# An mLSTM and expert-FFN kernel: a wait of its own for each row scatter, and a new order of the last silus and token rows

## The reference, cut to what matters

```python
xn = layernorm(x)
# attention, per sequence and head
q, k, v = headwise(xn, wq), headwise(xn, wk), headwise(xn, wv)
D_mat = exp(log_D - max_log_D)               # from the forget and input gates, causal
C = (q @ k.T / sqrt(dh)) * D_mat
h = (C / (maximum(abs(C.sum(-1)), exp(-max_log_D)) + eps)) @ v
s = multihead_layernorm(h) * (1 + ln_w)
# experts
top1 = argmax(softmax(xn @ router_w + router_b))
for i in range(8):                            # each token keeps its expert's result
    a, g = split(xn @ w1[i] + b1[i])
    y_i = (a * sigmoid(g)) @ w2[i] + b2[i]
out = x + s * silu(y)
```

## Time and profile before

| | us |
|---|---|
| median of 3 runs | 234.85 (234.79 to 235.79) |
| the profiled execution's own time | 235.47 |
| its span, first to last instruction | 233.7 |
| TensorE busy | 217.2 (93% of the span) |
| VectorE busy | 162.4 (69%) |
| ScalarE busy | 140.3 (60%) |
| POOL busy | 92.6 (40%) |

### The profile page before, as it was taken

How to read it: one execution, slowest core, us unless ns; L and a number is a source line. 1 busy time by engine, 2 the same in 40 slices (tenths; PEclk the granted TensorE clock), 3 DMA queues, 4 the chain that set the end, 5 groups by cost and what they waited for, 6 DMA issues and landing times.

```text
span 233.7 us, 6082 instructions
## 1 busy us (share of the span) xinstructions
PE 217.2 (93%) x1824; PEld 173.1 (74%) x1834; DVE 162.4 (69%) x491; ACT 140.3 (60%) x326; POOL 92.6 (40%) x130
## 2 busy tenths in 40 slices
PE   8998989678899889999999999999999999998994
PEld 6787654234545454569999999999999999996541
DVE  5998699507467658755877987798779967963170
ACT  2398758456767676877556655665566555552044
POOL 5667930756566563000333333333433333335100
PEclk9999999976999999999999999999999999999999
DMA  6999999930179111400077021011101001000498
GB/s 180 328 363 418 337 205 210 209 111 34 49 202 327 35 48 44 129 3 28 18 223 255 14 67 57 23 57 56 47 28 52 22 26 35 17 22 13 110 341 267
DMA packets 23617, 29.26 MB, mean 125 GB/s; under 512 B 3319, under 2 KB 18687, under 8 KB 23585
## 3 DMA queue, kind: packets, MB, share of 16 engines
q1 hardware_dynamic: 18994, 20.42, 26.5%
q0 software_dynamic: 3424, 8.36, 14.5%
q10 hardware_dynamic: 1168, 0.10, 0.4%
HBM read 19.99 MB, written 9.34 MB: 126 GB/s over the span
## 4 chain that ended last, share of the span: by engine, by line
PE 73%; DVE 13%; issue 5%; ACT 2%; another core or an unknown queue 2%; DMA 2%; POOL 0%; DVEq 0%; SPq 0%; ACTq 0%
PE bank L1213 15%; PE bank L1222 15%; PE head_bank L1213 15%; PE head_bank L1171 5%; PE bank L1183 4%; DVE cm L876 4%; PE bank L1161 3%; DVE stats L711 2%; PE bank L1199 2%; PE head_bank L1141 2%; PE bank L1285 2%; DMA x_sb<-in_L_attn_x 2%; PE bank L1288 1%; PE head_bank L1285 1%
## 5 line engine op out<-in xcount | busy, mean ns | idle before, releaser
L450 POOL DMA_INDIRECT y_tokens<-ffn,idx x39 | 38.6, 991 | 88.1 <-DVE ffn L1004 87.5
L876 DVE TENSOR_TENSOR cm<-dm,head_bank 128x1024 f32<-128x1024 f32 (+1 forms) x32 | 29.1, 951 | 23.7 <-PE head_bank L1171 8.5
L444 POOL DMA_INDIRECT xs_sorted<-xn,pos x32 | 31.1, 973 | 28.0 <-PE head_bank L1171 10.5
L1222 PE MATMUL bank<-w_sb,dm 128*128 x312 | 41.3, 275 | 0.1
L1213 PE MATMUL bank<-xsT,wc 128*128 128x128 f32 x320 | 39.0, 275 | 0.0
L1222 PEld LDWEIGHTS bank<-w_sb,dm 128*128 128x128 f32 x312 | 38.0, 192 | 0.3 <-issue 0.3
L1213 PEld LDWEIGHTS bank<-xsT,wc 128*128 128x128 f32 x320 | 37.3, 192 | 0.0
L1213 PE MATMUL head_bank<-xsT,wc 128*128 128x128 f32 x304 | 37.0, 275 | 0.0
L1213 PEld LDWEIGHTS head_bank<-xsT,wc 128*128 128x128 f32 x304 | 35.5, 192 | 0.0
L586 ACT ACTIVATE wc<-w_sb 128x512 f32 x39 | 24.6, 630 | 14.4 <-issue 14.3
L565 ACT ACTIVATE dm<-bank 128x512 f32<-128x512 f32 x48 | 27.0, 597 | 8.1 <-PE bank L1161 7.5
(11 more groups left out here) (192 smaller groups left out, 345.5 us busy)
## 6 DMA issues: line engine op xcount, KB each, us to landing
x_sb<-in_L_attn_x SPq DMA_DIRECT2D x16, 256.0 KB, 5.1
w_sb<-in_L_ffn_w SPq DMA_DIRECT2D x8, 512.0 KB, 8.9
w_sb<-negated_rows POOLq DMA_DIRECT2D x8, 508.0 KB
xs_sb<-xs_sorted SPq DMA_DIRECT2D x13, 192.0 KB
xs_sorted<-b_sb SPq DMA_DIRECT2D x1, 2048.0 KB, 11.1
w_sb<-y_tokens SPq DMA_DIRECT2D x8, 256.0 KB, 4.4
out_x<-w_sb SPq DMA_DIRECT2D x8, 256.0 KB, 2.5
y_tokens<-ffn,idx POOLq DMA_INDIRECT x39, 2.3
```

The source lines that it names most:

```text
L444: pool.indirect_dma_start(xs_dram, bass.IndirectOffsetOnAxis(ap=pos[:, t:t + 1], axis=0), xn[:, t, :], None).then_inc(s_scat, 16)
L450: pool.indirect_dma_start(y_dram, bass.IndirectOffsetOnAxis(ap=idx[:, j:j + 1], axis=0), ys_sb[:, j // CH % 2, j % CH, :], None, bounds_ch ...
L876: dve.tensor_tensor(cm[:, b % 2, :, m0:m1, :], dm[:, b % 2, :, m0:m1, :], head_bank[:, :, m0 * P:m1 * P].rearrange("p h (m t) -> p h m t", ...
L1222: last = pe.matmul(bank[6 + j % 2][:, 0:D], uT[:, j % 2, c, :], w2_sb[:, bass.ds(e * (HC * D) + c * D, D)], start=(c == 0), stop=(c == HC ...
```

## The change

Three things, in POOL's, ScalarE's, VectorE's and TensorE's lists:

- `SCAT_AT` goes. POOL's scatters now go through b = 0 to 13: one waits for the first half of weighing b (`s_cm` 2b + 1), for b = 3, 6, 9 and 12 another for the copy of the value sums of b (`s_ute`), and one for the token rows of b (`s_oe`). That makes 28 + 4 = 32.
- The token rows of block 14 move, on TensorE and on ScalarE: TensorE's two transposes from behind `values_sum(14)` to behind `hidden(0)`, ScalarE's copy from behind `evac_u(14)` to behind `gate(0)`.
- In the last iterations `silu(36)` stands ahead of `product(38)` and `add_bias(37)`, `silu(37)` ahead of `add_bias(38)`, and ScalarE's sigmoid of block 36 ahead of `gate(38)`. (The sigmoid of ScalarE is now a function; its waits are the same.) The six calls' worth of idle products before the eighth product of x are removed.

```diff
--- before.py
+++ after.py
@@ -55,7 +55,7 @@
     TP = T // NPC
     NSTEPS = 25
     SQUARES_AT = {1: (0, 1), 8: (2,), 9: (3,), 16: (4,), 17: (5,), 24: (6,), 25: (7,)}
-    SCAT_AT = [t * 13 // T for t in range(T)]
+    THREE_IN = (3, 6, 9, 12)
     GT = 8
     EPS_LN = 1e-5
     EPS_N = 1e-8
@@ -438,11 +438,21 @@
             pool.wait_ge(s_id, 1)
             pool.wait_ge(s_fill, 32)
             pool.wait_ge(s_pos, 1)
-            for t in range(T):
-                if SCAT_AT[t] != (SCAT_AT[t - 1] if t else 0):
-                    pool.wait_ge(s_sc, SCAT_AT[t])
+            def scatter(t):
                 pool.indirect_dma_start(xs_dram, bass.IndirectOffsetOnAxis(ap=pos[:, t:t + 1], axis=0),
                                         xn[:, t, :], None).then_inc(s_scat, 16)
+
+            t = 0
+            for b in range((T - len(THREE_IN)) // 2):
+                pool.wait_ge(s_cm, 2 * b + 1)
+                scatter(t)
+                if b in THREE_IN:
+                    pool.wait_ge(s_ute, b + 1)
+                    scatter(t + 1)
+                pool.wait_ge(s_oe, b + 1)
+                scatter(t + 1 + (b in THREE_IN))
+                t += 2 + (b in THREE_IN)
+            assert t == T
 
             for j in range(NBLK):
                 pool.wait_ge(s_ye, j + 1)
@@ -614,6 +624,12 @@
                 act.activation(sg[:, j % 2, :, :].rearrange("p c t -> p (c t)"), bank[2 * (j % 2) + 1][:, :],
                                ACT.Sigmoid).then_inc(s_th, 1)
 
+            def sigmoid(j):
+                act.wait_ge(s_yb, j + 1)
+                if j >= 2:
+                    act.wait_ge(s_ye, j - 1)
+                act.activation(sy[:, j % 2, :], yb[:, j % 2, :], ACT.Sigmoid).then_inc(s_sy, 1)
+
             decay(0, 0)
             decay(0, 1)
             evac_q(6)
@@ -628,6 +644,7 @@
                 if b == B - 1:
                     act.wait_ge(s_cm, 2 * (B - 1))
                     gate(0)
+                    outputs(b - 1)
                 if b + 2 < B:
                     decay(b + 2, 0)
                 if b == B - 2:
@@ -636,7 +653,7 @@
                 if b + 2 < B:
                     decay(b + 2, 1)
                     decay(b + 2, 2)
-                if b + 1 < B:
+                if b + 2 < B:
                     outputs(b)
                 if b == 5:
                     act.wait_ge(s_seld, 1)
@@ -659,15 +676,14 @@
                     evac_xs(j + 1)
                 if 2 <= j < NBLK - 1:
                     copy_w(j + 1)
+                if j == NBLK - 1:
+                    sigmoid(j - 2)
                 if 1 <= j < NBLK:
                     gate(j)
                 if j == 1:
                     outputs(B - 1)
-                if j >= 2:
-                    act.wait_ge(s_yb, j - 1)
-                    if j >= 4:
-                        act.wait_ge(s_ye, j - 3)
-                    act.activation(sy[:, j % 2, :], yb[:, j % 2, :], ACT.Sigmoid).then_inc(s_sy, 1)
+                if j >= 2 and j != NBLK - 1:
+                    sigmoid(j - 2)
                 for i in SQUARES_AT.get(j, ()):
                     squares(i)
 
@@ -1016,6 +1032,8 @@
                     if j >= 2:
                         copy_w(j + 1)
                         step(normals)
+                if j >= NBLK - 1:
+                    silu(j - 2)
                 if 1 <= j < NBLK:
                     product(j)
                     if j == 1:
@@ -1026,7 +1044,7 @@
                     token_index(j // CH)
                 if 1 <= j <= NBLK:
                     add_bias(j - 1)
-                if j >= 2:
+                if 2 <= j < NBLK - 1:
                     silu(j - 2)
                     step(normals)
             while step(normals):
@@ -1245,6 +1263,7 @@
                     pe.wait_ge(s_xone, 1)
                     pe.wait_ge(s_dm, 3 * B)
                     hidden(0)
+                    token_rows(b - 1)
                 if b + 2 < B:
                     log_decay(b + 2, 0)
                 if b == B - 2:
@@ -1280,8 +1299,6 @@
             pe.wait_ge(s_xr, 16 * NPC)
             pe.wait_ge(s_yb, NBLK)
             for g in range(NPC):
-                if g == NPC - 1:
-                    keep_warm(6, g)
                 pe.matmul(bank[g][:, :], ident[:, :], x_sb[:, g * TP:(g + 1) * TP, :], start=True, stop=False)
             for g in range(NPC):
                 pe.wait_ge(s_prod, g + 1)
```

## The result

The changed kernel takes 248.86 us (median of 4 runs, 248.16 to 249.91) against 235.32 for the one before in the same comparison: a ratio of 1.0562, 95% interval 1.0514 to 1.0609. The profiled execution took 248.84, its span 246.9, against 233.7 before: 13.2 us more. The forecast of 235.9 and its range (to 239.0) were both too low.

The account below looks back on a forecast made before the run. Three parts with different limits: attention stretched by scatters, block loop by TensorE, end by TensorE beside nearly full DMA. Terms -4.7 + 5.2 + 2.3 - 0.5 - 1.3 = +1.0 gave 235.9 us from the median, range 231.5 to 239.0.

Parts of the forecast that it names:

- W1 to W2: Attention stage, between starts of VectorE's weighings 1 and 2: burst of eight scatters goes, 3.7 us instead of 8.84.
- The four triples: Attention steps beside three scatters in a row: four at 4.65 us each, 18.6 in all, as before.
- rival C: Attention scatters: five back to back at four places, longer runs, slower by 2.4 to 4.8 us, 239.0; chance 0.18.
- The steps behind them: Attention steps with pairs of scatters right behind the triples: four at 3.21 us, 12.8 in all.
- The five other pairs: Attention steps beside two scatters, not behind a triple: five at 3.47 us, 17.4 in all.
- The forget rows: Two small transposes that only block 3 of the attention has: 0.4 us added to its step.
- Sorted rows: End of attention: TensorE's turning of sorted rows waits for the last scatter and loads, W15 (weighing 15) + 5.1: +5.2 us.
- Clock: Behind the stall at the turning: TensorE falls to its lower clock level, +2.3 us.
- token rows: Block 14's token rows moved: TensorE's wait for the value sums is filled with block 0, -0.5 us.
- Rival D: Behind the turning: the clock does not fall, or only while TensorE waits, 233.6 us; chance 0.14.
- The end: Last stage: silus let the last y scatters start 0.95 us earlier, idle products go; together -1.3 us.
- Rival B: Attention scatters hold up nobody, as in the block loop: 230.0 us, half of it 232.9; chance 0.28.

Follow-up runs that it names:

- e3: Changed kernel with two scatters a block, none by the copy of the value sums, the four left over behind the last pair: 244.36 us.
- e5: As e3, but each pair's first scatter waits for the next block's scores instead of this block's token rows, 0.2 us later: 243.93 us.
- e2: Changed kernel with all 32 scatters behind the last weighing, so none runs beside the attention stage: 272.47 us.
- e1: Changed kernel with the scatters of before, all by TensorE's scores, the rest of the change kept: ratio to before 0.9938.
- e12: The changed kernel itself again, on a chip where the kernel before took 223.1 us: 230.19 us, ratio 1.0288.
- e7: Changed kernel with y scatters in the block loop sent three in a row per chunk, last chunk excepted, attention untouched: 253.83 us.
- e6: As e3, but GpSimd clears a 128 x 384 tile between the two scatters of each pair: 234.99 us.
- e15: Changed kernel with 32 scatters in one stream, no waits for the attention, each behind a cleared 128 x 4 tile: 222.72 us, 0.9943 of before.
- e8: Changed kernel with five scatters at the start, then two an iteration in event order, none by the value sums' copy: 236.28 us, ratio 0.9993.

## Why the prediction was wrong, step by step

**W1 to W2**, put at 3.7: 2.96. The burst went as forecast, and 0.7 more with it. It was 5.6 us of hold.

**The four triples**, put at 4.65 each: the steps they stand in took 5.93, 7.30, 7.19 and 7.31, together 27.7 instead of 18.6. This is the step that failed most, +9.1. The groups do not stay as they were. I had seen that POOL waited for scores behind each triple, and priced the loss of that pause under rival C at 0.6 to 1.2 a triple. It costs 2.3 on average, because the row of five spans the end of the next block's scores, and in three of the four places their release moves to 1.9 to 2.0 behind the last start. C had the right mechanism and side, and its price of 239.0 was too low by 10.

**The steps behind them**, 12.8 put for four: 14.1 (3.45, 3.07, 3.79, 3.82). The prediction has no term for the clock inside the stage, and most of this is lost there. The last two stand at a granted clock of 0.50 (in the windows 93 to 95 and 106 to 109 us), each behind a held row in which TensorE had no products for 2.4 us, and their scores take 1.63 and 1.67 instead of 0.94. Behind the first row of over 7 us, where TensorE idled as long, the clock stayed at 1.00 and the step takes 3.07.

**The five other pairs**, 3.47 each, 17.4: 20.7 (4.61, 4.00, 4.00, 4.16, 3.97), +3.4. The 3.47 was one sample, of a pair that the scores had released. A pair released by the token rows starts 0.2 earlier, and e3 against e5 showed that the second scatter then catches the value sums. "As before" was wrong by those 0.2 us. The forget rows, put at 0.4, are 0.56 (e2: 3.76 against 3.20). In sum the thirteen steps took 62.6 instead of 49.2, and W15 came 12.9 later than forecast, where it should have been 4.7 ahead of before.

**Sorted rows**, put at +5.2: +4.2 in the profile of after, since W15 itself was late and the last scatter started 0.91 ahead of it, not just behind. Where nothing is held it is +5.20. From the last scatter's start to the load it took 2.27 (2.50 put), from there to the turning 2.70 (2.6 put). The Trainium skill (DMA: Bandwidth & Descriptors, section Anatomy of one DMA — SWDGE (gpsimd) path) gives a fixed 2.0 us and the bytes at 436 GB/s for a DMA that GpSimd issues. Applied to the scatter, and to SP's load as well, which that section doesn't cover, it comes to an estimate of 4.6; the trace has 4.97.

**Clock**, put at +2.3, and **token rows** at -0.5: the right mechanism, and nearly the size. From the turning to the second block it is 4.33 in e1 against 4.90 before, so the token rows gave 0.57; and 7.22 in the changed kernel against 4.33 in e1, so the clock cost 2.9 (2.6 in e12). Rival D fell.

**The end**, put at -1.3: -1.47 in this profile, but from the second block to the end the sixteen other profiles with the loop and the end of the change range from 126.5 to 128.6, with a median of 127.1, against 127.92 before: -0.9 is the better figure. Of the silus' 0.95 the trace shows half: the last y scatter starts 4.83 behind the start of the last products (230.39) instead of 5.34. It follows its silu by 0.77, as forecast, but silu 38 itself comes 0.45 later against those products than before. "Silu 37 costs bias 38 nothing" was wrong by that: bias 38, behind silu 37 now, starts 0.48 later. What the idle products gave was not measured by itself.

**Rival B**, scatters that hold up nobody, put at 230.0 to 232.9, fell for the chip of the result: e3, e5 and e7 show the hold with releases by VectorE, ScalarE and TensorE. Its argument from the block loop was wrong in the cause: it is the distance of 2.79 us that makes the y scatters harmless, not VectorE's release. On the later chips its premise is true, for the kernel before as well, so the change has nothing to win there and costs 7 us (2.9%, from two runs).

So with a hold the change loses 8.1 in the scatters and 6.5 at the turning; without one only the 7 at the turning. The waits for an event of its own were to break up a burst. They did, a gain of 5.9 us, and made four rows of five, each across a release of scores. The four steps beside these take 27.7 us; they take 13.3 without scatters (e2) and were forecast at 19.0 with the forget rows.

What stays open: what holds the releases, and whether at TensorE or on the way to the engines that wait; why chips differ (each was used at one time only, so chip and time weren't separated); and the best schedule where they are held. e6 shows that 28 scatters can pass for 1.2 us; with e1's rest and an early end this should win most of the 12.6 us, but no such kernel was run there.

## What to carry to other kernels

Price a wait that is moved by what its queue then does in a row, not by the event alone: list the order on the engine, mark where several entries become ready together, and look at what the row covers. A cost read from one sample (a pair, 3.47) belongs to that sample's phase as well. And before a schedule is tuned around a stall, run the same kernel on more than one chip: here 12 of 235 us were a property of where, or when, it ran.

## What the runs showed of the hardware that was not expected

- Beside scatters of GpSimd that follow each other 1.27 us apart, TensorE's products run on time and its releases don't. A release that falls due just ahead of the second scatter's start comes 0.76 behind that start (e3). In three steps of the changed kernel and eight chunks of e7 one that is due beside the third or a later one comes 1.7 to 2.0 behind the start of the last (75.85 - 73.84, 145.49 - 143.61). This does not hold everywhere: in the burst of eight before, the value sums' release comes at 47.79, 0.65 behind the start of the sixth scatter (47.14), with two more to follow. Due 0.25 ahead of the second, a release comes 0.03 behind its start (e5), which is 1.30 behind the first one's. A single scatter costs next to nothing: 0.15 from the value sums to their copy in e6 and e8, against 0.06 where nothing is held. That copy comes 1.37 behind the scatter's start. In a row the next scatter starts at 1.27, before it; whether this is what makes a row special was only argued.
- On four of the six chips of the experiments none of this is there. The kernel before, with the same scatters of 0.97 us, takes 223 instead of 235 us there, with steps equal to those of a stage without scatters to 0.03 us.
- The wait of 4 to 5 us at the turning was followed in the changed kernel, on both kinds of chip, by a granted clock of 0.50, the lower of the two levels (1.2 GHz), for about 6 us of work, though TensorE was busy for 4.00 of 4.00 us in the window from 116 to 120. In e12 the clock was 1.00 ahead of that wait; in the profile of the changed kernel above it had been low once already, from 106 to 109. Where the rows were in time (e1, e15) no such stretch stands behind the turning.
